# Three words placed later in the hand-written order of an attention and expert kernel: the transposes of the second pair of head groups, of the normalised heads, and the projection

## What is computed

```python
xn  = layernorm(x)
q, k, v = split_heads(xn @ Wq + bq), split_heads(xn @ Wk + bk), split_heads(xn @ Wv + bv)   # 16 heads of 8
q, k = rope(q), rope(k)
att = softmax(causal(q @ k.T / sqrt(8)))
y   = merge_heads(att @ v) @ Wp + bp                  # heads -> Y -> W in the kernel
x   = x + layernorm(y)
h   = layernorm(x)
out = x + layernorm(experts(h, top 2 of 16) + shared_expert(h))
```

## Time and profile before

| | us |
|---|---|
| median of three runs | 1203.71 |
| the profiled execution's own time | 1194.12 |
| its span (first to last instruction) | 1192.2 |
| PE busy | 1055.7 (89%) |
| DVE busy | 836.7 (70%) |
| POOL busy | 830.8 (70%) |
| ACT busy | 724.7 (61%) |
| granted PE clock, mean over the span | 0.962 |

### The profile page before, as it was taken

The page is one execution under the profiler, slowest core; times in us unless marked ns, Lnnn a source line. Parts: engine busy times, 40 slices in busy tenths (PEclk is TensorE's granted clock), DMA queues, the critical chain, the costliest instruction groups (busy, mean ns, idle before and its releaser), DMA issues.

```text
span 1192.2 us, 27197 instructions
## 1 busy us (share of the span) xinstructions
PE 1055.7 (89%) x8652; PEld 667.2 (56%) x8652; DVE 836.7 (70%) x2235; ACT 724.7 (61%) x1603; POOL 830.8 (70%) x976
## 2 busy tenths in 40 slices
PE   3479999999999999999999999998778888888896
PEld 2345556565565655656656556555446666666642
DVE  5487988878788787787888877753645555555534
ACT  5137777768677686776776877775234444444435
POOL 6455768889788788887888876766635555555557
PEclk8579999999999999999999999998889999998999
DMA  5442432431433314323243133336423333333276
GB/s 90 118 138 63 134 94 67 138 117 60 113 97 119 109 60 127 119 81 115 65 139 109 62 112 112 70 85 149 119 75 114 117 113 108 113 115 102 92 228 201
DMA packets 109750, 129.93 MB, mean 109 GB/s; under 512 B 17723, under 2 KB 90412, under 8 KB 105004
## 3 DMA queue, kind: packets, MB, share of 16 engines
q1 hardware_dynamic: 100908, 110.04, 32.6%
q0 software_dynamic: 8704, 18.17, 4.4%
HBM read 80.99 MB, written 45.50 MB: 106 GB/s over the span
## 4 chain that ended last, share of the span: by engine, by line
PE 74%; DVE 6%; ACT 4%; issue 3%; POOL 2%; DMA 1%; another core or an unknown queue 0%; SPq 0%; POOLq 0%; ACTq 0%; DVEq 0%
PE wide L1484 15%; PE heads_ps L1573 13%; PE wide L1711 11%; PE score L1484 9%; PE wide L1538 6%; DVE mx L1356 4%; PE score L1550 4%; PE score L1685 3%; PE wide L1694 2%; PE wide L1695 2%; ACT values L1003 2%; PE wide L1744 1%; PE wide L1746 1%; PE wide L1745 1%; PE wide L1639 1%
## 5 line engine op out<-in xcount | busy, mean ns | idle before, releaser
L1003 ACT ACTIVATE values<-score 128x512 f32<-128x512 f32 (+1 forms) x704 | 369.6, 559 | 108.2 <-PE score L1484 98.2
L1356 DVE TENSOR_REDUCE mx<-wide 128x2 f32<-128x1024 f32 (+3 forms) x384 | 389.2, 1041 | 59.8 <-PE wide L1484 55.4
L1484 PE MATMUL score<-qk 75*128 75x384 bf16 (+5 forms) x1216 | 230.7, 311 | 7.2 <-ACT values L1003 6.2
L915 POOL TENSOR_SCALAR_AFFINE_SELECT values<-values 128x512 f32<-128x512 f32 x256 | 163.4, 648 | 100.5 <-ACT values L1003 98.8
L960 POOL DMA_INDIRECT token_scratch<-spread,e_id x144 | 138.2, 960 | 128.4 <-issue 69.1
L1484 PE MATMUL wide<-qk 72*128 72x128 bf16 (+3 forms) x2152 | 212.8, 249 | 14.0 <-DVE mx L1356 8.9
L1484 PEld LDWEIGHTS wide<-qk 72*128 72x128 bf16 (+1 forms) x2152 | 136.5, 99 | 108.1 <-DVE mx L1356 36.8
L1573 PE MATMUL heads_ps<-values 128*32 128x512 f32 (+3 forms) x2048 | 173.9, 440 | 0.3 <-POOL values L915 0.3
L904 POOL DMA_INDIRECT sorted_scratch<-zr,places x128 | 135.5, 1059 | 50.1 <-issue 26.3
L1711 PE MATMUL wide<-qk,xnT 128*128 x288 | 116.7, 488 | 31.7 <-ACT xnT L1085 30.0
L1484 PEld LDWEIGHTS score<-qk 75*128 75x128 bf16 (+1 forms) x1216 | 88.6, 98 | 81.8 <-issue 34.1
(11 more groups left out here) (188 smaller groups left out, 1841.3 us busy)
## 6 DMA issues: line engine op xcount, KB each, us to landing
qk<-parts_scratch SPq DMA_DIRECT2D x192, 192.0 KB
parts_scratch<-spread SPq DMA_DIRECT2D x16, 768.0 KB
qk<-sorted_scratch SPq DMA_DIRECT2D x144, 66.5 KB
front<-token_scratch SPq DMA_DIRECT2D x16, 512.0 KB, 5.1
xt<-attn_x SPq DMA_DIRECT2D x16, 256.0 KB
xr<-attn_x SPq DMA_DIRECT2D x16, 256.0 KB
x_scratch<-z SPq DMA_DIRECT2D x16, 256.0 KB
shared_scratch<-s_out SPq DMA_DIRECT2D x16, 256.0 KB
```

The source lines that it names most:

```text
L915: nc.gpsimd.affine_select(out=prob[n][:, :, 0:P], in_=prob[n][:, :, 0:P], compare_op=ALU.is_ge, fill=0.0, base=0, pattern=[[0, HG], [1, P] ...
L1003: nc.scalar.activation(free_ap(prob[kb][:, hs_[0], :], [[1, N * len(hs_)]]), score[SCORE_RING.buffer(b, step)][:, 0:N * len(hs_)], ACT.Exp ...
L1356: nc.vector.tensor_reduce(mx[:, h0:h0 + len(hs_), j:j + 1], src, axis=AX.X, op=ALU.max).then_inc(p1_max, 1)
L1484: last = nc.tensor.matmul(out[at:at + width], weights[:, at:at + width], moving, start=start, stop=stop)
```

## The change

On one line of the string `heads1@-1` moves from behind `rnormal` to behind `s0.7`. `Y` moves from before `v0.0` to behind `s1.0`, and `W` from before `mask2.3 s1.2` to behind `s1.2`. No other word moves, and nothing else is edited. The new order holds for every engine that has a share in the word.

```diff
-    "s0.0 v3.1@-1 mask2.1 s0.1 p18@0 s0.2 p19@0 s0.3 v3.2@-1 v3.3@-1 p20@0 s0.4 s0.5 rnormal heads1@-1 p21@0 mask2.2 "
-    "s0.6 s0.7 p22@0 s0.8 K p23@0 s0.9 place s0.10 cos Y v0.0 M1@0 s1.0 s1.1 N1@0 p0 W mask2.3 s1.2 rstd s1.3 v0.1 H2 "
+    "s0.0 v3.1@-1 mask2.1 s0.1 p18@0 s0.2 p19@0 s0.3 v3.2@-1 v3.3@-1 p20@0 s0.4 s0.5 rnormal p21@0 mask2.2 "
+    "s0.6 s0.7 heads1@-1 p22@0 s0.8 K p23@0 s0.9 place s0.10 cos v0.0 M1@0 s1.0 Y s1.1 N1@0 p0 mask2.3 s1.2 W rstd s1.3 v0.1 H2 "
```

## The result

The changed kernel takes 1210.18 us, the median of five runs (1208.66 to 1229.97). The kernel before took 1203.45 us beside it (1201.42 to 1205.51). The ratio is 1.0058, 95% interval 1.0036 to 1.0080: 0.6% slower. The forecast was 1204.5 with a range of 1199.5 to 1208.5, so the time lies outside it, on the slower side.

A forecast was written before the change was run, and what follows sets the result against it. The chain runs through PE for three quarters of the span, so moves pay only where PE stands still. Fifteen passes times 0.05 us add 0.8 to the median 1203.7, giving 1204.5 us, range 1199.5 to 1208.5.

The forecast's parts named there:

- Steps 1 to 4: PE's wait moves from `heads1` to `s0.6`; `heads1` starts 0.92 us later; `K` waits 0.45 us, replacing `Y`'s wait.
- The sign that the prediction set: On PE, `v0.1` stays as far behind the copy of `oT` as now, 8.50 us, if the forecast is right.
- Steps 5 and 6: From `v0.0` to `s1.3`: `yT` ready about 414.8, just before PE arrives at `W`; `v0.1` starts between 416.22 and 416.29.
- The rival in which `W` stops: PE stops at `W` for a late `yT`: 15 x 0.3 = 4.5 us on top of 0.8, 1209.0; chance 0.19.
- The term of +0.05 us a pass: Later start of `v0.1` on PE in each pass: 15 passes times 0.05 give +0.8 us.
- The prediction's walk: Step-by-step timeline of one pass on PE: `v0.1` would start between 416.22 and 416.29, against 416.20 now.
- the Trainium skill's constant for an isolated matmul: 398 cycles at 2.4 GHz, about 0.16 us more per PE stop; 15 times 0.16, 2.4 us, not added.
- A stop itself costs PE nothing extra here.: After idle time `p21` starts 0.49 us behind `heads1`, without it 0.50, so no price for a stop.
- I take it as given for both kernels: What holds back `v3.3`, ahead of the `oT` copy and `heads1`, is unknown and assumed the same in both.
- the hold of `v3.3`: Slow `v3.2` and `v3.3` before the `oT` copy: 16 matmuls take 2.12 us, 24 later ones 1.50; PE idles 1.24.
- The rival in which the waits shrink: `K` need not stop, so passes keep `v0.0`'s gain: 15 x 0.40 = 6 us, 1197.7, in the extreme 1192; chance 0.20.

The follow-up runs named there:

- e1_heads: Kernel before with only `heads1` moved, to behind `s0.7`; `Y` and `W` stay. 1210.33 us, ratio 1.0062 to the kernel before on chip A.
- e2_yw: Kernel before with only `Y` and `W` moved; `heads1` stays. 1197.42 us, ratio 0.9969 to the kernel before on chip A.
- e3: Changed kernel plus four useless 512-column matmuls in the stop ahead of `s0.6`. 1206.14 us, ratio 1.0045 to the kernel before on chip A.
- e11: Changed kernel plus two useless ACT copies ahead of the `oT` copy and eight useless matmuls ahead of `s0.6`. 1212.82 us, ratio 1.0156 to before, chip C.
- e6: Changed kernel run again without further edit, on chip B. 1122.97 us, ratio 1.0002 to the kernel before on that chip.
- e13: Changed kernel with POOL's scatters `d6` and `d7` moved to behind `mask0.0`. 1178.56 us, ratio 0.9863 to the kernel before on chip D.
- e16_after: Changed kernel run again without further edit, on chip D. 1211.35 us, ratio 1.0102 to the kernel before on that chip.
- e15: Kernel before with POOL's scatters `d6` and `d7` moved to behind `mask0.0`. 1178.74 us, ratio 0.9883 to the kernel before on chip D.
- e14: Kernel before with `Y` and `W` moved, and scatters `d6` and `d7` moved to behind `mask0.0`. 1177.23 us, ratio 0.9864 to the kernel before on chip D.
- e12: Kernel before with POOL's scatters `d6` and `d7` moved to behind `mask0.0`, on chip C. 1178.41 us, ratio 0.9888 to the kernel before on that chip.
- e9_before_held: Kernel before plus two useless 0.60 us ACT copies ahead of the second pair's `oT` copy. 1223.88 us, ratio 1.0259 to the kernel before, chip C.

## Why the prediction was wrong

**Steps 1 to 4, the new waits.** Right. `s0.6` waits for ACT and `K` for `y`. In the passes with the full stop `heads1` starts 2.67 us behind `s0.4` instead of 1.72, so 0.95 later (0.92 forecast), and `K` stands idle for 0.38 us (0.45 forecast). The sign that the prediction set, `v0.1` 8.50 us behind the copy to `oT`, was 8.59 in the two such passes whose clock stayed up, and 9.64 to 11.17 in the four whose clock fell.

**Steps 5 and 6, `W` just in time.** Right. There is no wait at `W` in the pass shown, and one of 0.2 us in the whole loop. The rival in which `W` stops gave a time near the measured one, 1209.0, and is refuted: its wait does not exist. A right number would have been no evidence for it.

**The term of +0.05 us a pass.** It is 0.10 to 0.11 (47.35 against 47.25 without the late copy, and `v0.1` 8.30 instead of 8.20 behind `s0.5` in the passes without a stop): 1.6 us over 15 passes instead of 0.8, which is small beside the loss. The prediction's walk itself ended 0.02 to 0.09 later, and its upper end was nearly right. With an estimate from the Trainium skill's constant for an isolated matmul (TensorE: Matmul & The Clock Gate, "Single matmul latency") it would have been 0.05 + 0.16 = 0.21. The measured value lies between, and no run here separates that constant from the rest.

**"A stop itself costs PE nothing extra here."** This step failed. It was judged by the spacing of two matmuls right behind a stop, and that is true as far as it goes. It says nothing of the clock that is granted one or two microseconds later. The sum had no term for the clock at all, though the profile's page has a line for it and the mean was 0.962. The runs put in its place: five stretches of 3.4 to 6.8 us at 1.2 GHz in the loop, 20.5 us together. The first four cost 7.1 us and the fifth 1.5, which is 8.6 of the loop's 9.7 us in the profiled executions, and more than the whole difference of the medians, 6.7.

**What makes the clock fall is shown only in part.** Moving `heads1` is enough (three stretches in e1_heads, none in e2_yw). The stop ahead of `s0.6` is needed: where it is filled with work (e3, e11) or absent (e6, e13), the clock falls at most once between 100 and 800 us. The second stop, ahead of `K`, is not needed. Counted over the kernel after, e1_heads and e16_after, 11 stretches between 100 and 800 us follow a stop ahead of `s0.6` of 1.08 to 1.16 us, and five of them begin before PE has reached `K`, which then finds no stop. Nor is there more idle time in sum: 1.24 and 0.29 us a pass before, 1.10 and 0.38 after. So why 1.10 us ahead of `s0.6` can lower the clock, while 1.21 to 1.31 us ahead of `heads1` never did in the traces of before and e2_yw, stays open.

**"I take it as given for both kernels"** (the hold of `v3.3`). The chain's 2.12 us for the 16 matmuls reach to the start of the copy; PE's timeline gives them 0.86 us. Harmless for the sum of the waits, but it hid that the loss depends on it. With it the change costs 0.6% and 1.0% (two chips); without it 0.02% (chip B) and nothing measurable (e13 against e15 on chip D).

**The rival in which the waits shrink.** Half of it was true and went unseen: `Y` and `W` alone give 0.3% on chip A. In the whole change `heads1` takes that back even where the clock stays up (0.10 us a pass more in e13, 0.25 less in e14), and the clock comes on top.

**What else stays open.** Which chips have the late copy and why: the first one, A, C and D have it, B doesn't, with the same scatters and loads beside each other. Whether the scatters alone would do it, without SyncE's loads, wasn't tried. Nor does a run say why among passes with the full stop some keep their clock, as the one from 507.55 does, and some lose it, or why the last pass loses it in some kernels (e3, e12, e15) and not in others (before, e13).

## What to carry to other kernels

Moving a word past a stop of PE can lower the granted clock even though the waits in sum stay the same. No wait shows it, so look at the length of one matmul form and at the clock in windows of one pass. Before moving words around a stop, find out what makes it. Here the cause was a neighbour on another engine's list, and moving that was worth 1.1 to 1.2%, where the change lost 0.6 to 1.0%. Test a theory of the clock with useless matmuls inside a stop; outside a stop they are plain work.

## What the runs showed of the hardware

- **The clock behind short stops.** Beside the 1.24 us ahead of `heads1` the clock stayed at 2.4 GHz in all passes of the kernel before. With 1.10 to 1.17 us ahead of `s0.6` it fell to 1.2 GHz in four of six such passes of the changed kernel, in two of them before PE reached `K`. With useless copies that made the stop ahead of `heads1` some 2.35 us long in eight passes and shorter in the others (e9_before_held), it fell nine times between 100 and 800 us; the pass at 420 us, with 2.37 us, kept its clock.
- **Completions late beside indirect scatters.** On the first chip and on A, C and D the end of `v3.3` reached ACT up to 1.3 us late (a wait of 1.51 us instead of 0.22) while POOL issued scatters, and PE went on issuing meanwhile. On B it did not.
- **Chips differ by more than the edits.** The kernel before took 1122.46 us on chip B and 1192.58 to 1203.45 on the others. The late copies are some 15 us of that (705.8 instead of 720.5 between copies). Most of the rest lies behind the loop: 311.0 us from the last copy to the end in e6_after_again, 367.3 in e13_after_d67, for kernels whose loops both take 705.8. Nothing here says why.
